# The pass for the maxima of the attention scores: 16 fills of two full matmuls, or 8 fills of four row tiles of 32 rows

## The chip, the cores and the metric

The kernel runs on one core of one Trainium2 chip. The metric is the device time of one execution in microseconds (us); three executions of the kernel before took 3145.16, 3150.84 and 3152.6 us, median 3150.84 us. The profile is of one execution more, whose own time is 3152.29 us and whose span, from the first to the last instruction, is 3150.6 us.

## The reference

A batch of 32 latent arrays of 64 x 256 (float32) passes through six residual layers; the context has 1601 keys of 256 values for each of the 32. The layers are a cross attention with one head, a causal self attention, a quantised feed-forward layer with a convolution, a cross attention with 16 heads, a causal self attention with 16 heads, and a mixture of 8 experts of which each token takes two. Only the fourth is touched here:

```python
def _L1_xattn_ref(x, mem, W_kv, W_q, W_proj, b_proj):
    kv = (mem @ W_kv).reshape(B, Nkv, 2, HEADS, HEAD_DIM)      # 16 heads of 16
    k = kv[:, :, 0].transpose(0, 2, 1, 3)
    v = kv[:, :, 1].transpose(0, 2, 1, 3)
    q = (x @ W_q).reshape(B, Nq, HEADS, HEAD_DIM).transpose(0, 2, 1, 3)
    attn = jnp.einsum('bhqd,bhkd->bhqk', q, k) * SCALE
    attn = jax.nn.softmax(attn, axis=-1)                       # over 1601 keys
    out = jnp.einsum('bhqk,bhkd->bhqd', attn, v)
    return out.transpose(0, 2, 1, 3).reshape(B, Nq, C) @ W_proj + b_proj
```

The softmax needs, for each of the 16 x 64 pairs of head and query of one batch element, a shift near the largest of 1601 scores. The kernel finds these maxima in a pass of its own (scores with one fp32r product, layout: queries on partitions), and then computes the scores again, accurately, with keys on partitions, for the exponentials.

## The kernel before

The 32 batch elements are worked on in 16 pairs; a pair is one trip (`pe_pair`) and each of its two elements is one call of `pe_batch(n, ...)`, n = 0 or 1. Trips 1 to 14 are one hardware loop (L1302); the first and the last stand outside it. The order of each engine's instructions is written out by hand, engine by engine, and semaphores tie them together.

One `pe_batch` on TensorE (L1237) is, in order:

1. waits for the split queries (`qbd_hi`, `qbd_lo`) and keys of this element and, where there is a next element, for its split context (`ctx_lo`);
2. the maxima stage, 16 units u. Unit u takes head pair u // 2 (2 heads x 64 queries = 128 output partitions) and one half of the keys: two matmuls (512 and about 290 columns) of 128 x 128 weights `qbd_hi`. These weights are block diagonal by head: in the 128 rows of a group of eight heads, head pair j has values only in rows 32 j to 32 j + 31, and zeros elsewhere. The output fills banks 0 and 1 or banks 2 and 3 in turn, so a unit waits for the reduction of the unit before the last (`mx_red >= u - 1`, L1137);
3. between the units stand the projections of the next element's keys and values (`project`, "pieces": 8 key pieces of 6 matmuls of 400 columns, then 7 value pieces, six of 12 and the last of 6 matmuls of 256 columns), twelve of the fifteen; the last tile of the weighted values of the element before (`weigh(1 - n, 12)`) after unit 0, and its denominators (`end_batch`, one matmul into bank 7) after unit 2;
4. a transposition of the maxima (`m8`, L1260 and L1261), the other three pieces, and then the wait for `shift` (L1267);
5. the scores stage: 13 tiles of keys (L1268), each with 2 + 12 matmuls in row tiles of 64 rows, the exponential on ScalarE, `weigh` (16 products in column tiles of 32 columns), and steps of the next layer (`finish`) and of the next pair (`prepare`).

`project` writes banks 6 and 5 in turn. ScalarE takes each piece out (`evac`, L749), and copies the sums of the weighted values (`copy_sums`) after the first piece.

VectorE in the maxima stage (`maxima`, L1619): for each unit it waits for `mx_ps`, reduces 802 or 799 columns of two banks to one column of `mpart` (L1626), and after unit 2 does `end_batch` (reciprocal L1614 and product L1616). Then it reduces `mpart` to `m8` (L1630), waits for its transposition, and builds `shift` (L1632 to L1642) for the scores.

Of the kernel before, what the change touches and what calls it, by code (L numbers as in the profile page):

```python
# [19 lines left out]
ALU = mybir.AluOpType  # L20
# [5 lines left out]
AX = mybir.AxisListType.X  # L26

P = 128
B, S, D = 32, 64, 256
NK = 1601  # L30
NKP = NK + 1
# [30 lines left out]

MAX_CHUNKS = [(0, 512), (512, HALF - 512), (HALF, 512), (HALF + 512, NKP - HALF - 512)]
PROJ_CHUNKS = [(0, HALF - 400), (HALF - 400, 400), (HALF, 400), (HALF + 400, NKP - HALF - 400)]
CTX_PARTS = 2
MAX_UNITS = 2 * PAIRS

K_PIECES = [("k", o, c) for o in range(KT) for c in range(len(PROJ_CHUNKS))]
V_PIECES = [("v", t, min(t + 2, KEY_TILES)) for t in range(0, KEY_TILES, 2)]
PIECES = K_PIECES + V_PIECES  # L70
PIECE_AFTER = (0, 2, 3, 4, 5, 7, 9, 10, 12, 13, 15)
CTX_STEPS = (1, 2, 6, 7)
# [43 lines left out]
def build(nc, io, out):  # L116
    ctx = ExitStack()
    with ctx:
# [91 lines left out]
        sideB = sb_b("sideB", [P, 3584])  # L210
        mpart = sb_b("mpart", [P, PAIRS, 2])
        sh8 = sb_b("sh8", [P, 2, P], BF16)
# [709 lines left out]
        def _(pe):  # L922
# [210 lines left out]
            def maxima(n, u):  # L1133

                pair, half = divmod(u, 2)
                if u >= 2:
                    pe.wait_ge(s.mx_red, T["mx"].now() + u - 1)  # L1137
                for c, width in MAX_CHUNKS[2 * half:2 * half + 2]:
                    at = 1024 * ((u + 1) % 2) + c - HALF * half
                    at = PS[:, at:at + width]  # L1140
                    mm = pe.matmul(at, qbd_hi[:, n, pair // 4, (pair % 4) * P:(pair % 4) * P + P], k_hi[:, n, pair // 4, c:c + width],  # L1141
                                   start=True, stop=True)
                mm.then_inc(s.mx_ps, 1)
# [15 lines left out]
            def end_batch(n, fin):  # L1159

                pe.wait_ge(s.sums_ready, T["sums"].up())
                if n == 0 and fin:
                    pe.wait_ge(s.p4T_ready, T["p4T"].now() + 1)
                pe.matmul(bank(7, D), spread[:, :, :].rearrange("p j d -> p (j d)"), sums_sb[:, :], start=True, stop=True).then_inc(s.den_ps, 1)
# [72 lines left out]
            def pe_batch(n, first, last):  # L1237
# [6 lines left out]
                if ahead:  # L1244
                    pe.wait_ge(s.ctx_lo_ready, T["ctxB"].up(KT * CTX_PARTS))
                for u in range(MAX_UNITS):
                    maxima(n, u)
                    if not (first and n == 0):
                        if u == 0:
                            weigh(1 - n, KEY_TILES - 1)  # L1250
                        if u == 2:
                            end_batch(1 - n, not first)
                    if ahead and u in PIECE_AFTER:
                        project(pieces.pop(0), 1 - n)
                T["mx"].up(MAX_UNITS)
                if ahead:
                    project(pieces.pop(0), 1 - n)

# [131 lines left out]
        def _(v):  # L1390
# [228 lines left out]
            def maxima(b, first):  # L1619

                for u in range(MAX_UNITS):
                    pair, half = divmod(u, 2)
                    width = HALF if half == 0 else NK - HALF
                    at = 1024 * ((u + 1) % 2)
                    v.wait_ge(s.mx_ps, T["mx"].up())
                    v.tensor_reduce(mpart[:, pair, half:half + 1], PS[:, at:at + width], AX, ALU.max).then_inc(s.mx_red, 1)  # L1626
                    if u == 2 and not (first and b == 0):
                        end_batch(1 - b)
                v.wait_ge(s.mx_red, T["mx"].now())
                v.tensor_reduce(m8[:, :, 0:PAIRS], mpart[:, None, :, :].broadcast_to([P, 4, PAIRS, 2]), AX, ALU.max).then_inc(s.m8_ready, 1)  # L1630
                v.wait_ge(s.m8T_ps, T["m8T"].up())
# [317 lines left out]
```

## Time and profile before

| | |
|---|---|
| median of three executions | 3150.84 us (3145.16 to 3152.6) |
| profiled execution, its own time | 3152.29 us |
| its span | 3150.6 us |
| mean granted TensorE clock | 0.918 of full speed |
| TensorE busy | 2665.3 us, 85% |
| VectorE busy | 1537.9 us, 49% |
| ScalarE busy | 1409.4 us, 45% |
| GpSimd busy | 926.9 us, 29% |
| part with the cross attention of 16 heads (first to last matmul of the maxima) | 689.3 to 2546.1 us |

Times in the rows are microseconds from the start of the span. "busy" of a matmul runs to its modelled end, which overlaps the next one's start; the step from one start to the next is the rate. PE is TensorE, PEld its weight loads, DVE VectorE, ACT ScalarE, POOL GpSimd. PEclk is the granted TensorE clock, 1.00 for 2.4 GHz and 0.50 for 1.2 GHz.

### The profile page before, as it was taken

What the parts mean: (1) busy time and instruction counts of PE and PEld (TensorE: products, weight loads), DVE (VectorE), ACT (ScalarE), POOL (GpSimd) and SP (SyncE); (2) the same over time, 40 slices, a digit from 0 to 9 for tenths busy, and PEclk for the clock granted to TensorE, in tenths of its full rate; (3) what the DMA queues carried; (4) which work ended last, traced back from release to release, by engine and by line L of the source; (5) the groups of instructions that cost most, each with busy time, mean ns of one, the idle gap of its engine ahead of it and who ended that gap; (6) DMA issues with size and microseconds to landing.
All of it is one profiled execution on the core that took longest, in us unless ns stands there. A gap on an engine that the chain in (4) does not pass through costs nothing.

```text
span 3150.6 us, 76656 instructions
## 1 busy us (share of the span) xinstructions
PE 2665.3 (85%) x31988; PEld 2234.6 (71%) x31988; DVE 1537.9 (49%) x2629; ACT 1409.4 (45%) x2563; POOL 926.9 (29%) x867
## 2 busy tenths in 40 slices
PE   6999722359999999999999999999999975499997
PEld 3555411158888888788788788788788854499997
DVE  3444477723543543444454344345345334377775
ACT  1222211136546546546545545545555521356554
POOL 1000043353333333333343342432433301312111
PEclk9999855679999999999999999999999975799999
DMA  8888400031001001001101100100110001466665
GB/s 340 314 322 320 162 0 0 7 120 44 23 23 44 22 23 37 29 23 33 34 23 33 34 23 22 44 23 22 34 33 22 13 2 55 160 210 201 204 206 151
DMA packets 48609, 270.65 MB, mean 86 GB/s; under 512 B 4896, under 2 KB 23584, under 8 KB 33696
## 3 DMA queue, kind: packets, MB, share of 16 engines
q1 hardware_dynamic: 40160, 255.82, 22.4%
q0 software_dynamic: 8160, 10.29, 2.1%
q8 instruction: 265, 4.34, 0.6%
q14 instruction: 24, 0.20, 0.0%
HBM read 247.58 MB, written 20.61 MB: 85 GB/s over the span
## 4 chain that ended last, share of the span: by engine, by line
issue 41%; PE 24%; POOL 21%; DVE 6%; DMA 5%; ACT 2%; POOLq 1%; SPq 0%; DVEq 0%; ACTq 0%
POOL k_lo L530 7%; POOL ctx_lo L538 6%; PE PS L1025 3%; PE PS L1005 3%; POOL sideB L558 2%; DMA sum_d<-scaled,xg 2%; DMA unit_raw<-in_experts 2%; POOL qbd_lo L543 2%; PE PS L1357 2%; PE PS L1358 1%; PE PS L1359 1%; PE PS L1277 1%; PE PS L1153 1%; POOL slots_d L633 1%; DVE small L1508 1%
## 5 line engine op out<-in xcount | busy, mean ns | idle before, releaser
L1626 DVE TENSOR_REDUCE mpart<-PS 128x1 f32<-128x802 f32 (+1 forms) x512 | 486.7, 987 | 549.4 <-PE PS L1141 549.4
L825 ACT ACTIVATE probs<-PS 128x1024 f32<-128x1024 f32 (+1 forms) x416 | 425.4, 1023 | 252.5 <-PE PS L1277 246.8
L530 POOL TENSOR_TENSOR k_lo<-sideB,k_hi 128x400 fp32r<-128x400 f32 (+1 forms) x256 | 252.2, 985 | 469.8 <-ACT k_hi L761 469.7
L538 POOL TENSOR_TENSOR ctx_lo<-ctx_raw,ctx_hi 128x801 fp32r<-128x801 f32 x128 | 224.4, 1763 | 459.1 <-ACT ctx_hi L773 459.0
L1141 PE MATMUL PS<-k_hi,qbd_hi 128*128 128x512 f32 (+2 forms) x1024 | 274.3, 371 | 85.6 <-issue 48.2
L1277 PE MATMUL PS<-qbd_hi,k_hi 64*128 64x256 f32 (+1 forms) x1664 | 312.9, 373 | 0.0
L760 ACT COPY sideB<-PS 128x400 f32<-128x400 f32 (+1 forms) x256 | 126.4, 494 | 364.5 <-PE PS L1121 355.0
L1153 PE MATMUL PS<-probs,vals 128*32 128x64 f32 x13312 | 277.9, 225 | 1.7 <-ACT probs L825 1.7
L1141 PEld LDWEIGHTS PS<-k_hi,qbd_hi 128*128 128x128 f32 x1024 | 184.6, 200 | 114.0 <-issue 77.7
L1153 PEld LDWEIGHTS PS<-probs,vals 128*32 128x32 f32 x13312 | 209.8, 112 | 67.0 <-issue 16.2
L1128 PE MATMUL PS<-wkv_hi,ctx_hi 128*128 128x256 f32 (+1 forms) x832 | 236.8, 285 | 0.0
L1277 PE MATMUL PS<-qbd_hi,k_lo 64*128 64x256 f32 (+1 forms) x1664 | 235.4, 279 | 0.0
L1277 PE MATMUL PS<-qbd_lo,k_hi 64*128 64x256 f32 (+1 forms) x1664 | 235.0, 279 | 0.1
L1130 PE MATMUL PS<-wkv_hi,ctx_lo 128*128 128x256 f32 (+1 forms) x832 | 234.7, 282 | 0.0
L1129 PE MATMUL PS<-wkv_lo,ctx_hi 128*128 128x256 f32 (+1 forms) x832 | 233.6, 281 | 0.0
L1357 PE MATMUL PS<-xT_hi,unit_hi 128*128 128x256 f32 x736 | 209.2, 284 | 3.3 <-DVE xT_lo L1832 3.0
L1119 PE MATMUL PS<-ctx_hi,wkv_hi 128*128 128x400 f32 (+1 forms) x512 | 194.1, 379 | 18.9 <-POOL ctx_lo L538 18.9
L1358 PE MATMUL PS<-xT_lo,unit_hi 128*128 128x256 f32 x736 | 209.2, 284 | 0.0
L763 ACT COPY vals<-PS 128x512 f32<-128x512 f32 x192 | 112.8, 588 | 214.4 <-PE PS L1130 214.4
L1359 PE MATMUL PS<-xT_hi,unit_lo 128*128 128x256 f32 x736 | 208.5, 283 | 0.0
L1120 PE MATMUL PS<-ctx_lo,wkv_hi 128*128 128x400 f32 (+1 forms) x512 | 183.5, 358 | 0.0
L1121 PE MATMUL PS<-ctx_hi,wkv_lo 128*128 128x400 f32 (+1 forms) x512 | 183.3, 358 | 0.0
(319 smaller groups left out, 6151.6 us busy)
## 6 DMA issues: line engine op xcount, KB each, us to landing
unit_raw<-in_experts SPq DMA_DIRECT2D x46, 1536.0 KB, 7.1
ctxN<-in_ctxN SPq DMA_DIRECT2D x16, 3328.0 KB, 10.9
ctxT<-in_ctxT SPq DMA_DIRECT2D x16, 3204.0 KB, 10.4
ctx_raw<-in_ctxT SPq DMA_DIRECT2D x64, 801.0 KB, 4.4
slots_d<-pad_rows SPq DMA_DIRECT2D x2, 2990.0 KB, 18.6
xg<-slots_d SPq DMA_DIRECT2D x23, 260.0 KB, 2.8
x<-in_x SPq DMA_DIRECT2D x1, 2048.0 KB, 10.3
sum_d<-x SPq DMA_DIRECT2D x1, 2048.0 KB, 6.3
```

Source lines behind the costliest of these rows:

```text
L530: g.tensor_tensor(k_lo[:, n, a, c:c + width], k_raw[p % 2][:, 0:width], k_hi[:, n, a, c:c + width].bitcast(F32), ALU.subtract).then_inc(s. ...
L538: g.tensor_tensor(ctx_lo[:, a, cols], ctx_raw[:, cols], ctx_hi[:, a, cols].bitcast(F32), ALU.subtract).then_inc(s.ctx_lo_ready, 1)
L825: act.activation(probs[rows, t % PROBS, :], PS[rows, 1024 * (t % 2):1024 * (t % 2) + 1024], ACT.Exp).then_inc(s.pr_ready, 1)
L1128: pe.matmul(to, ctx_hi[:, k, keys], wkv_hi[:, k, D:2 * D], start=k == 0, stop=False)
L1130: mm = pe.matmul(to, ctx_lo[:, k, keys], wkv_hi[:, k, D:2 * D], start=False, stop=k == KT - 1)
L1141: mm = pe.matmul(at, qbd_hi[:, n, pair // 4, (pair % 4) * P:(pair % 4) * P + P], k_hi[:, n, pair // 4, c:c + width], start=True, stop=True)
L1153: mm = pe.matmul(bank(4, S, slice(32 * j, 32 * j + 32), g * S), vals[rows, n, mine:mine + 32], probs[rows, t % PROBS, at_head(h):at_head(h ...
L1277: mm = pe.matmul(bank(2 * (t % 2) + r, 256, rows, a * 256), keys_part[part, n, a, keys], queries[part, n, a, r * 256:r * 256 + 256], start ...
L1357: pe.matmul(to, hi[:, k, cols], tokens_hi[:, k, :], start=k == 0, stop=False)
L1358: pe.matmul(to, hi[:, k, cols], tokens_lo[:, k, :], start=False, stop=False)
L1359: mm = pe.matmul(to, lo[:, k, cols], tokens_hi[:, k, :], start=False, stop=k == KT - 1)
L1626: v.tensor_reduce(mpart[:, pair, half:half + 1], PS[:, at:at + width], AX, ALU.max).then_inc(s.mx_red, 1)
```

## The change

The maxima stage has 8 units instead of 16. Unit u takes a group a = u // 4 of eight heads and a quarter part = u % 4 of the keys (`PROJ_CHUNKS`: 402, 400, 400, 400 columns). Its four matmuls have 32 rows of weights each, rows 32 j to 32 j + 31 for head pair j, the only rows where that pair's weights are not zero, and write banks 0 to 3. One VectorE instruction then reduces all four banks to four columns of `mpart`. Every unit uses all four banks, so unit u waits for the reduction of unit u - 1.

The first piece and the last `weigh` of the element before now stand ahead of unit 0 and two waits are added ahead of them (`x_done`, `cat_ready`, since the piece writes bank 6); `end_batch` stands after unit 1; ten pieces stand after the units (1, 1, 1, 2, 1, 2, 1, 1), and the four that are left stand after the transposition of the maxima.

```diff
-MAX_CHUNKS = [(0, 512), (512, HALF - 512), (HALF, 512), (HALF + 512, NKP - HALF - 512)]
 PROJ_CHUNKS = [(0, HALF - 400), (HALF - 400, 400), (HALF, 400), (HALF + 400, NKP - HALF - 400)]
-MAX_UNITS = 2 * PAIRS
+MAX_UNITS = 8
-PIECE_AFTER = (0, 2, 3, 4, 5, 7, 9, 10, 12, 13, 15)
+PIECES_AFTER = (1, 1, 1, 2, 1, 2, 1, 1)
-        mpart = sb_b("mpart", [P, PAIRS, 2])
+        mpart = sb_b("mpart", [P, PAIRS, 4])
             def maxima(n, u):
-                pair, half = divmod(u, 2)
-                if u >= 2:
-                    pe.wait_ge(s.mx_red, T["mx"].now() + u - 1)
-                for c, width in MAX_CHUNKS[2 * half:2 * half + 2]:
-                    at = 1024 * ((u + 1) % 2) + c - HALF * half
-                    at = PS[:, at:at + width]
-                    mm = pe.matmul(at, qbd_hi[:, n, pair // 4, (pair % 4) * P:(pair % 4) * P + P], k_hi[:, n, pair // 4, c:c + width],
-                                   start=True, stop=True)
+                a, part = divmod(u, 4)
+                if u:
+                    pe.wait_ge(s.mx_red, T["mx"].now() + u)
+                c, width = PROJ_CHUNKS[part]
+                for j in range(4):
+                    rows = slice(32 * j, 32 * j + 32)
+                    mm = pe.matmul(bank(j, width), qbd_hi[rows, n, a, j * P:j * P + P], k_hi[rows, n, a, c:c + width], start=True, stop=True)
                 mm.then_inc(s.mx_ps, 1)
@@ pe_batch
+                if n == 0 and not first:
+                    pe.wait_ge(s.x_done, T["x_done"].now())
+                if n == 1 and not first:
+                    pe.wait_ge(s.cat_ready, T["cat"].now() + 1)
+                if ahead:
+                    project(pieces.pop(0), 1 - n)
+                if not (first and n == 0):
+                    weigh(1 - n, KEY_TILES - 1)
                 for u in range(MAX_UNITS):
                     maxima(n, u)
-                    if not (first and n == 0):
-                        if u == 0:
-                            weigh(1 - n, KEY_TILES - 1)
-                        if u == 2:
-                            end_batch(1 - n, not first)
-                    if ahead and u in PIECE_AFTER:
-                        project(pieces.pop(0), 1 - n)
+                    if u == 1 and not (first and n == 0):
+                        end_batch(1 - n, not first)
+                    if ahead:
+                        for _ in range(PIECES_AFTER[u]):
+                            project(pieces.pop(0), 1 - n)
                 T["mx"].up(MAX_UNITS)
-                if ahead:
-                    project(pieces.pop(0), 1 - n)
@@ maxima on VectorE
-                    pair, half = divmod(u, 2)
-                    width = HALF if half == 0 else NK - HALF
-                    at = 1024 * ((u + 1) % 2)
+                    a, part = divmod(u, 4)
+                    width = min(PROJ_CHUNKS[part][1], NK - PROJ_CHUNKS[part][0])
                     v.wait_ge(s.mx_ps, T["mx"].up())
-                    v.tensor_reduce(mpart[:, pair, half:half + 1], PS[:, at:at + width], AX, ALU.max).then_inc(s.mx_red, 1)
-                    if u == 2 and not (first and b == 0):
+                    v.tensor_reduce(mpart[:, 4 * a:4 * a + 4, part], PS[:, 0:2048].rearrange("p (j x) -> p j x", j=4)[:, :, 0:width],
+                                    AX, ALU.max).then_inc(s.mx_red, 1)
+                    if u == 1 and not (first and b == 0):
                         end_batch(1 - b)
                 v.wait_ge(s.mx_red, T["mx"].now())
-                v.tensor_reduce(m8[:, :, 0:PAIRS], mpart[:, None, :, :].broadcast_to([P, 4, PAIRS, 2]), AX, ALU.max).then_inc(s.m8_ready, 1)
+                v.tensor_reduce(m8[:, :, 0:PAIRS], mpart[:, None, :, :].broadcast_to([P, 4, PAIRS, 4]), AX, ALU.max).then_inc(s.m8_ready, 1)
```

## Rows read from the trace of the kernel before

**Rows 1.** Page, groups of instructions: count, busy, mean ns, idle before and its releaser.
```profile
L1626 DVE TENSOR_REDUCE mpart<-PS 128x1 f32<-128x802 f32 (+1 forms) x512 | 486.7, 987 | 549.4 <-PE PS L1141 549.4
```

**Rows 2.** Instructions in time, PE, one n = 1 element: start, duration, what, idle before.
```profile
1571.98 0.62 PE L1141 MATMUL PS<-k_hi,qbd_hi 128*128 128x512 f32 x2
1572.53 0.65 PE L1153 MATMUL PS<-probs,vals 65*32 65x64 f32 x32
1573.12 0.46 PE L1119 MATMUL PS<-ctx_hi,wkv_hi 128*128 128x402 f32 x1
...
1574.32 0.89 PE L1141 MATMUL PS<-k_hi,qbd_hi 128*128 128x512 f32 x4
...
1578.83 0.53 PE L1141 MATMUL PS<-k_hi,qbd_hi 128*128 128x512 f32 x2
1579.19 0.35 PE L1119 MATMUL PS<-ctx_hi,wkv_hi 128*128 128x400 f32 x1
...
1580.30 0.52 PE L1141 MATMUL PS<-k_hi,qbd_hi 128*128 128x512 f32 x2
...
1588.03 0.28 PE L1128 MATMUL PS<-wkv_hi,ctx_hi 128*128 128x256 f32 x1
...
1589.46 0.53 PE L1141 MATMUL PS<-k_hi,qbd_hi 128*128 128x512 f32 x2
```

**Rows 3.** Instructions in time, DVE, the same element.
```profile
1572.64 0.99 DVE L1626 TENSOR_REDUCE mpart<-PS 128x1 f32<-128x802 f32 x1 [2.29 <-PE PS L1141]
...
1576.69 1.75 DVE L1614 RECIPROCAL inv<-PS 128x256 f32<-128x256 f32 x1
...
1578.81 1.88 DVE L1626 TENSOR_REDUCE mpart<-PS 128x1 f32<-128x799 f32 x2
...
1591.82 1.89 DVE L1626 TENSOR_REDUCE mpart<-PS 128x1 f32<-128x802 f32 x2 [0.80 <-PE PS L1141]
1593.74 0.22 DVE L1630 TENSOR_REDUCE m<-mpart 128x32 f32<-128x64 f32 x1
1595.32 0.29 DVE L1632 TENSOR_SCALAR sh<-PS 128x128 bf16<-128x128 f32 x1 [1.35 <-PE PS L1261]
```

**Rows 4.** Instructions in time, PE, the end of the same stage.
```profile
1594.83 0.28 PE L1260 MATMUL PS<-ones 128*128 128x1 f32 x2
...
1599.13 0.39 PE L1273 MATMUL PS<-shift,onesb 64*128 64x512 bf16 x2 [0.31 <-DVE shift L1642]
```

**Rows 5.** Instructions in time, PE and DVE, the n = 0 element that follows.
```profile
1629.20 1.03 PE L1141 MATMUL PS<-k_hi,qbd_hi 128*128 128x512 f32 x2 [4.83 <-issue]
...
1631.18 0.70 PE L1119 MATMUL PS<-ctx_hi,wkv_hi 128*128 128x402 f32 x1
...
1633.35 1.54 PE L1141 MATMUL PS<-k_hi,qbd_hi 128*128 128x512 f32 x4
...
1658.79 0.39 PE L1273 MATMUL PS<-shift,onesb 64*128 64x512 bf16 x2 [0.31 <-DVE shift L1642]
...
1630.27 0.99 DVE L1626 TENSOR_REDUCE mpart<-PS 128x1 f32<-128x802 f32 x1 [20.57 <-PE PS L1141]
```

**Rows 6.** Instructions in time, PE, scores stage: pairs of row tiles of 64 rows.
```profile
1601.50 0.28 PE L1277 MATMUL PS<-qbd_lo,k_hi 64*128 64x256 f32 x2
1601.62 0.28 PE L1277 MATMUL PS<-qbd_hi,k_lo 64*128 64x256 f32 x2
```

**Rows 7.** Instructions in time, DVE: a reduction to four columns.
```profile
1567.81 0.69 DVE L1667 TENSOR_REDUCE small<-sideB 128x4 f32<-128x512 f32 x1
```

**Rows 8.** Windows: us, busy (instructions) of PE, PEld, DVE, ACT, POOL; PEclk; DMA share, GB/s.
```profile
1572.00:1595.00 23.00, 22.33 (x168) 20.65 (x166) 17.47 (x19) 9.85 (x22) 7.99 (x8) 1.00 0.01 1
1629.00:1636.00 7.00, 6.79 (x47) 5.42 (x48) 2.73 (x3) 1.17 (x3) 1.03 (x1) 0.51 0.01 2
2538.00:2540.00 2.00, 1.82 (x5) 0.98 (x4) 1.85 (x2) 0.00 (x0) 0.00 (x0) 0.50 0.00 0
```

**Rows 9.** Instructions in time, PE, the last element, which has no pieces.
```profile
2535.28 0.63 PE L1141 MATMUL PS<-k_hi,qbd_hi 128*128 128x512 f32 x2 [2.39 <-DVE mpart L1626]
```

## The prediction, made before the changed kernel ran

> **What bounds the kernel now.** I read the page's groups first. The reductions of the maxima on VectorE are its costliest group, 512 instructions, and VectorE idles 549.4 us in front of them, waiting for TensorE's fills [rows 1]; this says that TensorE leads in the stage, and no more, for most of that idle time is the scores stage ahead of each first fill. So I read the instructions in time through one maxima stage. In an n = 1 element the stage runs from 1571.98 (first fill) to 1599.13 (first matmul of the scores) [rows 2, 4], 27.15 us. TensorE is dense there: 22.33 us busy of 23.00, at the full clock [rows 8]. VectorE is busy 17.47 of those 23 us, so it is the second limit and not far behind: its last reduction ends at 1593.71, the maxima are ready at 1593.96 [rows 3], and TensorE gets to their transposition only at 1594.83 [rows 4], because pieces stand ahead of it. After the transposition the order turns round: TensorE waits 0.31 us for VectorE's `shift` [rows 4]. In an n = 0 element the stage starts after 4.83 us without a matmul and runs at half clock at first (0.51 over 7 us [rows 8]); it takes 1658.79 - 1629.20 = 29.59 us [rows 5].
>
> **The change, part by part.** Price list at full clock. A unit's fill of two matmuls takes TensorE 1579.19 - 1578.83 = 0.36 us; a key piece 1580.30 - 1579.19 = 1.11 us; a value piece 1589.46 - 1588.03 = 1.43 us, 0.119 for each of its 12 matmuls; the first piece after `weigh` 1574.32 - 1573.12 = 1.20; `weigh` 1573.12 - 1572.53 = 0.59 [rows 2]. From the start of a lone fill to the start of its reduction: 1572.64 - 1571.98 = 0.66 [rows 2, 3]. A reduction of 802 elements takes 0.99 alone and 0.92 back to back (0.99 + 0.92 give the 1.89 of two) [rows 3].
>
> *TensorE's work.* Removed: 16 fills, 5.8 us. Added: 8 fills of four matmuls. The trace has no row tile of 32 rows. It has pairs of row tiles of 64 rows: two matmuls of 256 columns start every 0.12 us [rows 6], where one after the other at the piece's rate (0.119 for 256 columns) would need 0.24. So row tiles run side by side and their weight loads keep up. One fill then lies between 0.18 us (all four side by side, 1.11 / 6 for 400 columns) and 0.74 (none); by the pairs' row I take 0.25. Eight make 2.0 us. Each fill also switches the array from 128 rows to row tiles and back. What a switch costs I read from the piece behind `weigh`: 1.20 against 1.11, about 0.1 us; the bound from below is nothing. 16 switches make 1.6 us. TensorE's work falls by 5.8 - 2.0 - 1.6 = 2.2 us for each element.
>
> *VectorE's work.* 802 elements take 0.99 [rows 3] and 512 elements in four groups 0.69 [rows 7], so 1.03 ns for each element more and nothing visible for groups. 1600 elements: 0.99 + 0.8 x 1.03 = 1.82 us; the bounds are 1.70 and 1.84, the latter twice the back-to-back 0.92. Eight make 14.6 us against 16 x 0.92 = 14.7. VectorE gains nothing.
>
> *The buffers.* This is the part that decides. Before, two halves of the four banks alternate and a fill lies beside a reduction. After, every fill uses all four banks: fill, reduction and fill stand in series. One round is a hop to TensorE (0.05), fill to reduction start, and 1.82. For the middle term: 0.66 is with two matmuls in series, 0.48 with one (less 0.18), and three more row tiles add 0 to 0.17 (three more weight loads at half of the 0.12 of a pair); with no overlap it is 0.48 + 3 x 0.18 = 1.03. I take 0.57. A round is 2.44 us, in which TensorE has 0.25 + 0.1 + 1.11 + 0.1 = 1.56 us to do where one piece stands behind the fill. So VectorE with its fills becomes the limit, and TensorE waits about 0.9 us in a round.
>
> *The sum for n = 1,* from the start of the stage. First piece and `weigh`, now ahead of unit 0: 1.20 + 0.59 = 1.79; VectorE has nothing to do in them, where before its first reduction started at 0.66. Eight rounds without the first hop: 8 x 2.39 + 7 x 0.05 = 19.47. `end_batch` after unit 1: from its reciprocal to the next reduction 1578.81 - 1576.69 = 2.12 [rows 3], which takes the place of one gap of 0.62: 1.50. Two pieces stand behind units 3 and 5: 0.25 + 0.1 + 2.22 + 0.1 = 2.67 and, with one value piece, 2.99, over a round of 2.44: 0.2 + 0.5 = 0.7. The last reduction ends at 1.79 + 19.47 + 1.50 + 0.70 = 23.5 (before: 21.7). `m8` has twice the input, 0.22 + 0.07 [rows 3]; at 23.8 TensorE starts the transposition, which it now waits for (before: 22.85). Then four pieces instead of three, 42 matmuls x 0.119 = 5.0, and 0.2 for the transposition and 0.1 for a switch: scores at 29.1. VectorE's chain to `shift`, 1599.13 - 1594.83 = 4.3 [rows 4], ends earlier, at 28.1, so here the fourth piece is late instead. The change costs 29.1 - 27.15 = 2.0 us.
>
> *n = 0.* The first piece and `weigh` now run at half clock: 1633.35 - 1631.18 = 2.17 [rows 5] and 1.0 (between 0.59 and twice that, since the small products of `weigh` do not all follow the clock). Fill to reduction start at half clock is 1630.27 - 1629.20 = 1.07 less one matmul of 0.33 = 0.74 [rows 5]. The first reduction starts at 3.2 + 0.74 = 3.9 instead of 2.36, 1.6 later than in n = 1: scores at 29.1 + 1.6 = 30.7 against 29.59, 1.1 us more.
>
> *Ends.* The first element (no `weigh`, no `end_batch`) about 1.5. The last has no pieces; before, its 16 reductions stand almost back to back, and eight rounds at half clock (2.61) with their gaps cost about 3. Total 15 x 2.0 + 15 x 1.1 + 1.5 + 3 = 51 us. Added to the profiled execution's own 3152.3 this is 3203; that execution lies 1.5 us above the median of the three, which does not matter here.
>
> *What costs nothing.* The added waits: `cat_ready` asks for a product that VectorE did one or two key tiles earlier, `x_done` for one of ten tiles earlier; behind each stands the whole of TensorE's queue, so an error here would cost every element its length. The 0.53 us that TensorE waited for the copied sums goes, but off the limit. ScalarE (9.85 busy of 23) and GpSimd (7.99) [rows 8] follow the pieces at 1 us each.
>
> *A rule of the skill.* That TensorE's gain is lost in emptying the banks is what rows 3 give above. The Trainium skill, TensorEngine Tiling, "PSUM Bottleneck", says that tiling speeds up TensorE but not the emptying of PSUM, which may then be the limit; the row agrees, 0.99 us for 802 elements whatever filled them. The Trainium skill, TensorE: Matmul & The Clock Gate, "The mechanism", puts row tiles 4 ns apart; by it fill to reduction start would be 0.49, an estimate of 0.6 us less for each element and 3184 in all. No row here shows four tiles, so the sum stays at 0.57.
>
> **The rivals.**
>
> *A, faster: TensorE stays the limit.* If the rounds were short enough to fit TensorE's work, its 2.2 us saved would count and the 0.5 of the wait for the sums: 31 x 2.5 = 78, 3075 us. The place is the gap between two reductions; it decides when a round is below about 2.1 us. For it: TensorE is the dense engine now. Against it: a reduction alone is 1.82 by two rows, and a matmul's pipeline from start to release is 0.48 before anything is added.
>
> *B, the clock.* After unit 2's fill and piece TensorE has nothing until the reduction behind `end_batch`: about 2.4 us idle. In the last element before there is such a hole, 2.39 us [rows 9], and the granted clock is 0.50 in the stretch behind it [rows 8], the lower level, 1.2 GHz, and stays there with fills alone. With pieces around it TensorE is busier than there, which speaks against. If it falls, two key pieces behind unit 3 take 4.3 instead of 2.2, a delay of about 2 us for each element: 3203 + 31 x 2 = 3265.
>
> *C, four tiles do not run side by side.* Then fill to reduction start is 1.03: 8 x 0.46 x 32 = 118 more, 3321. Rows 6 show it for two tiles only.
>
> *D, the last part of the stage is mis-sized* (reduction of 1.70, tiles at 0.48, switches at nothing): 8 x (0.12 + 0.09) = 1.7 and 0.2 less for each element, 3203 - 60 = 3143, no change. It needs all bounds at one end.
>
> **How the numbers follow.** Forecast 0.55, A 0.12, B 0.17, C 0.06, D 0.10. The time is 3203. Its own range, with the fill at 0.48 to 0.65 and the reduction at 1.75 to 1.84, is 3203 - 37 to 3203 + 25. Towards B (holes that fall in some of the elements only) the range goes to 3270; downwards to 3155, which leaves out A, C and a part of D. A measurement can tell about 0.3% (9 us) from no change. Faster: A and a third of D, 0.15. Same: a third of D and an edge of the forecast, 0.06. Slower: 0.79.
>
> **What would show it.** In the changed profile: reductions of 1.82 us with 0.6 us gaps before them put down to the fills of the maxima; waits of about 0.9 us of TensorE for `mpart`; four row tiles starting within 0.25 us; fill 0 about 1.8 us (n = 1) and 3.2 us (n = 0) into the stage; the scores 29.1 and 30.7 us after its start; no wait for `shift`; granted clock 1.00 through the n = 1 stage. A shorter gap or reduction shows A or D, a clock of 0.5 behind `end_batch` shows B, starts 0.18 us apart show C.

## The result, and the profile after

The changed kernel takes 3245.9 us (median of four, 3242.7 to 3248.6) against 3151.2, a ratio of 1.030 (95% interval 1.029 to 1.032): 3% slower. The forecast was 3203 within 3155 to 3270, slower with a chance of 0.79. The direction came as forecast, and so did the main mechanism, fill and reduction in series; the size was 95 us against 51, and most of the difference comes from the clock.

The page of the changed kernel, groups of instructions (columns as in [rows 1], which the first of these answers to):

```profile
L1627 DVE TENSOR_REDUCE mpart<-PS 128x4 f32<-128x1600 f32 (+2 forms) x256 | 467.4, 1826 | 656.4 <-PE PS L1140 656.4
...
L1140 PE MATMUL PS<-k_hi,qbd_hi 32*128 32x400 f32 (+1 forms) x1024 | 128.6, 491 | 119.5 <-DVE mpart L1627 119.4
```

VectorE does half the instructions at twice the length: 467 us busy against 487. The new row is the second. TensorE idles 119.4 us in front of the fills, and what releases it is the reduction. Before, its idle time there was a turn of the loop and 8 us of reductions.

Instructions in time, VectorE, in an n = 1 element of the changed kernel (answers to [rows 3]); its stage starts at 1617.30:

```profile
1619.65 1.83 DVE L1627 TENSOR_REDUCE mpart<-PS 128x4 f32<-128x1608 f32 x1 [3.99 <-PE PS L1140]
1622.05 1.83 DVE L1627 TENSOR_REDUCE mpart<-PS 128x4 f32<-128x1600 f32 x1 [0.56 <-PE PS L1140]
1623.79 1.75 DVE L1616 RECIPROCAL inv<-PS 128x256 f32<-128x256 f32 x1
...
1625.91 1.82 DVE L1627 TENSOR_REDUCE mpart<-PS 128x4 f32<-128x1600 f32 x1
1628.29 1.82 DVE L1627 TENSOR_REDUCE mpart<-PS 128x4 f32<-128x1596 f32 x1 [0.56 <-PE PS L1140]
...
1638.95 1.82 DVE L1627 TENSOR_REDUCE mpart<-PS 128x4 f32<-128x1596 f32 x1 [0.56 <-PE PS L1140]
1640.80 0.28 DVE L1632 TENSOR_REDUCE m<-mpart 128x32 f32<-128x128 f32 x1
```

Every reduction but the one behind `end_batch` (1625.91) has at least 0.56 us in front of it in which VectorE waits for a fill that could not start before the last reduction had ended; behind a double piece it is 0.97 and 1.26. A round is 1628.29 - 1625.91 = 2.38 us.

The same element on TensorE, fills alone:

```profile
1621.54 0.46 PE L1140 MATMUL PS<-k_hi,qbd_hi 32*128 32x400 f32 x4 [0.66 <-DVE mpart L1627]
1621.92 0.70 PE L1162 MATMUL PS<-sums,spread 128*128 128x256 f32 x2
...
1623.93 0.46 PE L1140 MATMUL PS<-k_hi,qbd_hi 32*128 32x400 f32 x4 [0.21 <-DVE mpart L1627]
...
1627.79 0.46 PE L1140 MATMUL PS<-k_hi,qbd_hi 32*128 32x400 f32 x4 [2.09 <-DVE mpart L1627]
```

Four matmuls of 400 columns fit in 0.38 us from their start to the next instruction (1621.54 to 1621.92), where two plain ones of together about 800 columns need 0.36 [rows 2]: the four row tiles do run side by side. The last row is the wait behind `end_batch`, which matters below.

The end of the stage in an n = 0 element (answers to [rows 4]):

```profile
1578.03 0.38 PE L1262 MATMUL PS<-ones 128*128 128x1 f32 x2 [0.62 <-DVE m L1632]
...
1583.48 0.39 PE L1275 MATMUL PS<-shift,onesb 64*128 64x512 bf16 x2
```

TensorE now waits for the maxima (0.62 us) and no longer for `shift`; between the two rows lie 5.45 us, 4.30 before.

Windows over whole stages, from the first piece to the first matmul of the scores. First the kernel before, n = 1 and n = 0:

```profile
1571.98:1599.13 27.15, 26.17 (x199) 24.24 (x198) 21.09 (x30) 11.91 (x26) 7.99 (x8) 1.00 0.00 1
1629.20:1658.79 29.59, 29.12 (x197) 26.61 (x198) 21.07 (x29) 11.20 (x24) 7.77 (x8) 0.89 0.01 1
```

and the changed kernel, two n = 1 and two n = 0 elements:

```profile
1617.30:1646.59 29.29, 24.73 (x199) 20.46 (x199) 20.66 (x22) 11.64 (x25) 7.77 (x8) 1.00 0.01 1
2249.58:2280.39 30.81, 26.23 (x200) 21.75 (x199) 20.67 (x22) 11.64 (x25) 7.78 (x8) 0.94 0.00 1
1676.51:1709.76 33.25, 29.47 (x195) 24.10 (x197) 20.88 (x21) 11.01 (x23) 7.76 (x8) 0.83 0.00 1
2310.45:2342.01 31.56, 28.45 (x195) 23.34 (x196) 20.49 (x21) 11.02 (x23) 7.97 (x8) 0.86 0.00 1
```

The same stage comes in several lengths, and the clock (the column after the five engines) goes with them. Added over all 32 elements, the stages are 896.1 us before and 992.4 after. The 992.4 count the last element, which has no pieces, from its first fill; with the `weigh` ahead of it, which before lay inside the stage, they are 993.0, 96.9 more. The spans differ by 96.3, so next to nothing moved outside the stages. Of the 96.9, n = 1 has 45.6 and n = 0 51.3. Of the n = 1 elements without the last, 15 in all, 8 are 29.3 us at clock 1.00 and 7 are 30.4 to 30.9 us at 0.94.

Windows of 2 us in the n = 0 element that starts at 1550.21, and the fill and the piece there:

```profile
1554.00:1556.00 2.00, 2.00 (x10) 1.83 (x6) 1.72 (x1) 0.03 (x1) 0.63 (x1) 0.50 0.00 0
...
1558.00:1560.00 2.00, 2.00 (x13) 1.49 (x13) 2.00 (x2) 0.58 (x2) 0.43 (x1) 1.00 0.00 0
1560.00:1562.00 2.00, 1.01 (x6) 0.68 (x4) 1.97 (x3) 1.19 (x3) 0.89 (x1) 1.00 0.00 0
1562.00:1564.00 2.00, 0.66 (x5) 0.46 (x6) 1.44 (x2) 0.01 (x1) 0.90 (x1) 1.00 0.00 0
1564.00:1566.00 2.00, 2.00 (x9) 1.99 (x9) 1.68 (x1) 0.63 (x2) 0.00 (x0) 0.70 0.00 0
1566.00:1568.00 2.00, 2.00 (x9) 1.19 (x9) 0.05 (x1) 0.89 (x3) 0.90 (x1) 0.50 0.00 0
```

```profile
1563.34 0.46 PE L1140 MATMUL PS<-k_hi,qbd_hi 32*128 32x400 f32 x4 [2.33 <-DVE mpart L1627]
...
1564.57 0.35 PE L1119 MATMUL PS<-ctx_lo,wkv_hi 128*128 128x402 f32 x1
...
1565.38 0.54 PE L1119 MATMUL PS<-ctx_lo,wkv_hi 128*128 128x400 f32 x1
```

TensorE had been idle 2.33 us; 1.5 us after it is back at work the clock falls from 2.4 to 1.2 GHz (0.54 for the matmul that took 0.35), and the two key pieces behind unit 3 run at half rate. The clock is low twice in this element: at its start, after the turn of the loop, and here. Over all elements with `end_batch` the second low stretch is seen in 7 of 15 n = 1 elements and in 11 of 15 n = 0 elements; "hit" below means such a stretch. Where it begins differs, from the last part of the wait itself to 1.7 us behind it.

### The profile page after: what moved, and what is told of

The parts are those of the page before. It is cut to its first block, busy times and chain, and to the rows that moved or that the text cites. A ratio compares the mean times of both kernels' runs of the same rounds, so it can differ in the third digit from the quotient of the medians.

```text
span 3246.9 us, 75907 instructions
## 1 busy us (share of the span) xinstructions
PE 2653.3 (82%) x31984; PEld 2143.6 (66%) x31988; DVE 1518.9 (47%) x2373; ACT 1411.3 (43%) x2563; POOL 924.6 (28%) x867
## 4 chain that ended last, share of the span: by engine, by line
issue 42%; PE 26%; POOL 20%; DVE 7%; DMA 3%; ACT 2%; POOLq 1%; SPq 0%; DVEq 0%; ACTq 0%
POOL k_lo L529 6%; POOL ctx_lo L537 6%; PE PS L1024 3%; PE PS L1004 3%; PE PS L1359 2%; PE PS L1360 2%; PE PS L1361 2%; POOL sideB L557 2%; DVE mpart L1627 2%; POOL qbd_lo L542 2%; DMA unit_raw<-in_experts 1%; PE PS L1279 1%; PE PS L1376 1%; PE PS L1378 1%; PE PS L1377 1%
## 5 line engine op out<-in xcount | busy, mean ns | idle before, releaser
L1627 DVE TENSOR_REDUCE mpart<-PS 128x4 f32<-128x1600 f32 (+2 forms) x256 | 467.4, 1826 | 656.4 <-PE PS L1140 656.4
L1118 PE MATMUL PS<-ctx_hi,wkv_hi 128*128 128x400 f32 (+1 forms) x512 | 228.4, 446 | 94.9 <-issue 53.2
L1140 PE MATMUL PS<-k_hi,qbd_hi 32*128 32x400 f32 (+1 forms) x1024 | 128.6, 491 | 119.5 <-DVE mpart L1627 119.4
L1118 PEld LDWEIGHTS PS<-ctx_hi,wkv_hi 128*128 128x128 f32 x512 | 111.8, 218 | 134.8 <-issue 128.0
L1119 PE MATMUL PS<-ctx_lo,wkv_hi 128*128 128x400 f32 (+1 forms) x512 | 198.4, 388 | 0.0
L1120 PE MATMUL PS<-ctx_hi,wkv_lo 128*128 128x400 f32 (+1 forms) x512 | 198.2, 387 | 0.0
```

Source lines behind the costliest of these rows:

```text
L1118: pe.matmul(bank(at, width), wkv_hi[:, k, cols], ctx_hi[:, k, c:c + width], start=k == 0, stop=False)
L1627: v.tensor_reduce(mpart[:, 4 * a:4 * a + 4, part], PS[:, 0:2048].rearrange("p (j x) -> p j x", j=4)[:, :, 0:width], AX, ALU.max).then_inc( ...
```

## The experiments

"Stages" are the sums over the 32 elements, read from instructions in time; the changed kernel has 992.4, the kernel before 896.1 (in the changed kernel and those made from it the last element is counted from its first fill). The medians are of 4 to 11 runs, beside the kernel before on the same chip (medians 3148.0 to 3150.0 us).

**Pieces into the wait behind `end_batch` (e1_hole).**

```diff
-PIECES_AFTER = (1, 1, 1, 2, 1, 2, 1, 1)
+PIECES_AFTER = (1, 1, 2, 1, 1, 2, 1, 1)
```

> Change: the pieces behind the eight units are (1,1,2,1,1,2,1,1) instead of (1,1,1,2,1,2,1,1), so two key pieces, 2.2 us, stand in front of the wait for the reduction that VectorE does only after end_batch; that wait was 2.33 us. Theory (the clock falls because of this hole, and costs about 1.6 us in some 20 of the 32 elements): the granted clock stays at 1.00 in the n = 1 stages and after the start of the n = 0 stages, and unit 3 no longer overruns its round by 0.4 us: 3246 - 20 x 1.6 - 30 x 0.4 = about 3202 us. Rival (the clock falls because the whole stage is less dense, or because of the row tiles, wherever the pieces stand): only the 0.4 us go, about 3234 us, and low clock is still seen in the stage.

Measured 3220.7 us (expected 3202, by the rival 3234), stages 963.3. The stage without a fall of the clock is 28.9 instead of 29.3, as expected. Three of 15 n = 1 elements (7 in the changed kernel) are still hit, at 29.6 to 31.2 us, and 12 of the 13 n = 0 elements behind a full turn of the loop are 31.1 to 31.9. So it lies between the two theories: the wait, 1.0 us instead of 2.1, still does harm at times, and the n = 0 elements did not lose what was expected.

**Matmuls that nobody reads, in that wait (e4_dummy).**

```diff
+                        if u == 2:
+                            pe.wait_ge(s.k_hi_ready, T["k_sb"].now() + 3)
+                            for _ in range(12):
+                                pe.matmul(bank(6, 256), wkv_hi[:, 0, 0:P], wkv_hi[:, 0, 0:256], start=True, stop=True)
```

> Change: in the changed kernel, twelve matmuls whose result nobody reads (256 columns, into the free bank 6, about 1.4 us at full clock) are added after the piece behind unit 2, in the wait for the reduction after end_batch. Nothing else moves. Theory (the hole makes the clock fall): although work is added, the low clock in the stages goes and the time falls by 20 x 1.6 us, to about 3213 us; unit 3 keeps its overrun of 0.4 us. Rival (the clock does not depend on this hole): 3246 us or a little more.

Measured 3205.2 us: 41 us less, with 372 matmuls added. In time on TensorE, and a whole n = 1 stage as a window:

```profile
1607.57 1.58 PE L1262 MATMUL PS<-wkv_hi 128*128 128x256 f32 x12
1609.81 0.46 PE L1140 MATMUL PS<-k_hi,qbd_hi 32*128 32x400 f32 x4 [0.67 <-DVE mpart L1631]
```

```profile
1599.33:1628.63 29.30, 26.18 (x210) 22.02 (x208) 20.67 (x22) 11.64 (x25) 7.77 (x8) 1.00 0.00 1
```

All 15 n = 1 elements are 29.3 us at clock 1.00, no one is hit. Nor is an n = 0 element hit behind the wait. The stages are 966.3, 26 less. Another 13 us lie outside the stages: the 14 stretches from an n = 1 element's scores to the next stage, 13 of them with a full turn of the loop, took 402.7 us in all against 415.4. The control shows what those are.

**The same matmuls elsewhere (e9_ctl).** Six behind unit 4 and six behind unit 6:

```diff
+                        if u in (4, 6):
...
+                            for _ in range(6):
+                                pe.matmul(bank(5 if u == 4 else 6, 256), wkv_hi[:, 0, 0:P], wkv_hi[:, 0, 0:256], start=True, stop=True)
```

> Control for e4_dummy: the same twelve matmuls that nobody reads for each element, so the same count of instructions, but six behind the piece of unit 4 and six behind that of unit 6, where TensorE waits only 0.5 to 0.8 us; the wait of 2.3 us behind end_batch stays open. Theory (e4_dummy was faster because its matmuls stood in the long wait): part of the n = 1 elements still show a stretch at half clock in the stage, as in the changed kernel, and the stages are not shorter than the changed kernel's 992 us in all; the time is 3246 us, less up to 14 us if the loop's turn, 30.0 us from scores to the next stage in the changed kernel and 29.0 in e4_dummy, goes with the count of instructions. Rival (any added matmuls keep the clock up, wherever they stand): stages of about 966 us in all and about 3205 us.

Measured 3242.6 us, stages 1003.5; the same 14 stretches took 402.8, as in e4_dummy. One n = 1 element, TensorE and the window:

```profile
1751.39 0.46 PE L1140 MATMUL PS<-k_hi,qbd_hi 32*128 32x400 f32 x4 [2.11 <-DVE mpart L1634]
1755.58 0.55 PE L1140 MATMUL PS<-k_hi,qbd_hi 32*128 32x402 f32 x4
```

```profile
1740.90:1772.05 31.15, 27.54 (x211) 23.30 (x210) 20.68 (x22) 11.64 (x25) 7.80 (x8) 0.95 0.01 1
```

13 of 15 n = 1 elements are hit (31.1 us at 0.95 against 29.7 at 1.00). So 13 us of e4_dummy's gain come with the added matmuls wherever they stand, and their place is worth 1003.5 - 966.3 = 37 us of stages. About 10 of these are rounds that the added matmuls make late here (29.7 against 29.3 at clock 1.00, 30 elements); the other 27 are what the open wait behind `end_batch` costs, 19 of them in the 13 n = 1 elements.

The 13 us are the idle time of TensorE at the turn. The first matmul of an n = 0 stage behind it, in the changed kernel and in e4_dummy:

```profile
1676.51 0.70 PE L1118 MATMUL PS<-ctx_hi,wkv_hi 128*128 128x402 f32 x1 [4.68 <-issue]
```

```profile
1657.85 0.70 PE L1118 MATMUL PS<-ctx_hi,wkv_hi 128*128 128x402 f32 x1 [3.97 <-POOL qbd_lo L542]
```

Over 13 turns the idle time is 4.77 us on average in the changed kernel and 3.80 and 3.81 in the two with added matmuls; all the rest of the stretch takes 25.24 us in each of the three. In the changed kernel TensorE mostly starts over a microsecond after its last input, `qbd_lo`, is there, and the profile puts the wait down to nothing but its own issue (11 of 13); with the added matmuls it starts 0.0 to 0.5 us after `qbd_lo`, which now ends the wait.

**A longer wait (e10_big), and the changed kernel again (a2_same).**

```diff
-PIECES_AFTER = (1, 1, 1, 2, 1, 2, 1, 1)
+PIECES_AFTER = (1, 2, 0, 2, 1, 2, 1, 1)
```

> Change against the changed kernel: the piece behind unit 2 stands behind unit 1 instead (pieces 1,2,0,2,1,2,1,1), where VectorE is busy with end_batch anyway; TensorE's amount of work and VectorE's row are the same, but TensorE's wait behind end_batch is one stretch of about 2.7 to 3.3 us instead of 2.3. Theory (a long enough wait makes the clock fall): more elements are hit, all n = 1 stages are 30.8 us or more instead of 6 or 7 of 15, about 3246 + 9 x 1.6 = 3260 us. Rival (the clock looks at the amount of work in the stage, not at one wait): the same as the changed kernel, 3246 us.

> The changed kernel once more, for a second trace: how many of its n = 1 elements are 29.3 us and how many 30.4 to 30.9. Theory (the fall of the clock hangs on how the wait behind end_batch lies against something that the kernel does not set): another number of elements is hit than the 6 of 15 in the first trace, and each hit costs 1.1 to 1.7 us. Rival (it hangs on the data or on the place in the program): the same elements are hit again.

e10_big measured 3251.1 us, stages 1002.1, with waits of 2.56 us; 11 of 15 n = 1 elements are hit, not all, so the expectation failed in its strong form. a2_same measured 3245.8 us and has 10 of 15 hit; the first n = 1 element is hit in the first trace and not in the second, the third the other way round. So the same program at the same place is hit or not: the place in the program alone does not decide a single case. A wait of 2.6 us cannot be told from one of 2.1 by these counts.

**All 128 rows (e2_full).**

```diff
-                    rows = slice(32 * j, 32 * j + 32)
-                    mm = pe.matmul(bank(j, width), qbd_hi[rows, n, a, j * P:j * P + P], k_hi[rows, n, a, c:c + width], start=True, stop=True)
+                    mm = pe.matmul(bank(j, width), qbd_hi[:, n, a, j * P:j * P + P], k_hi[:, n, a, c:c + width], start=True, stop=True)
```

> Change: same eight units, banks and reductions, but each of the four matmuls of a unit has all 128 rows of weights (96 of them zeros) instead of 32, so the four run one after the other. Theory (four row tiles run side by side and shorten the gap between two reductions): fill to reduction start rises from 0.51 to about 1.06 us, 8 x 0.55 = 4.4 us for each element, 3246 + 32 x 4.4 = about 3386 us, less up to 33 us if the denser stage keeps the clock up. Rival (the row tiles bring nothing, the changed kernel's 0.51 us is latency): within 10 us of 3246.

Measured 3335.2 us. VectorE in time:

```profile
1669.27 1.82 DVE L1626 TENSOR_REDUCE mpart<-PS 128x4 f32<-128x1596 f32 x1 [1.09 <-PE PS L1139]
```

The gap is 1.09 instead of 0.56, so the four tiles take 0.53 us out of a round. n = 1 stages are 32.3 at clock 1.00 against 29.3, 3.0 more and not 4.4: `end_batch` covers one gap of eight, and the two behind double pieces were late anyway (1.11 and 1.46 us against 0.97 and 1.26). These 1.4 us in 30 elements are the larger part of what the time is under the expected 3386.

This kernel turned out to bear on two other steps. Its wait behind `end_batch` is 1.8 us, and 6 of its 15 n = 1 elements are hit, such as this one, 33.8 us against 32.3:

```profile
1787.18:1820.98 33.80, 28.65 (x198) 26.30 (x197) 20.68 (x22) 11.63 (x25) 7.77 (x8) 0.95 0.00 1
```

So the fall behind the wait does not need row tiles. The slow start does differ: over the first 12 us of the 13 n = 0 stages that follow a full turn of the loop, its TensorE spends 5.7 us at half clock on average; the changed kernel, with the same order of work, 8.0.

**Three pieces behind the transposition (e3_tail).**

```diff
-PIECES_AFTER = (1, 1, 1, 2, 1, 2, 1, 1)
+PIECES_AFTER = (1, 1, 1, 2, 1, 2, 1, 2)
```

> Change: two pieces instead of one behind unit 7, so three pieces instead of four stand behind the transposition of the maxima. Theory (the last part of the stage is set by TensorE's four pieces, 5.4 us, where VectorE's chain to the shift needs 4.3): the transposition is 0.65 us later, the rest 1.15 shorter, 31 x 0.5 = 15 us less, about 3231 us, and TensorE again waits for the shift. Rival (the transposition's place is what counts, VectorE's chain hangs on it): 0.65 later and nothing back, about 3266 us.

Measured 3233.2 us (expected 3231). An n = 1 stage at clock 1.00 is 28.8 instead of 29.3, the 0.5 that was expected. 11 of 15 n = 1 elements are hit here, at 29.9 to 31.3 us, with the same wait of 2.1 us, so the total came close to the forecast with more falls in n = 1 than in the changed kernel and, as the stages of n = 0 show (499 us against 516), with less lost there.

**Nothing ahead of unit 0 but `weigh` (e5_first), and both together (e7_combo).**

```diff
-PIECES_AFTER = (1, 1, 1, 2, 1, 2, 1, 1)
+PIECES_AFTER = (1, 1, 3, 1, 1, 2, 1, 1)     # e7_combo: (1, 1, 3, 1, 1, 2, 1, 2)
-                if ahead:
-                    project(pieces.pop(0), 1 - n)
                 if not (first and n == 0):
                     weigh(1 - n, KEY_TILES - 1)
```

> Change against the kernel e1_hole: the first piece no longer stands ahead of unit 0 but behind unit 2, in what is left of the hole (pieces 1,1,3,1,1,2,1,1 behind the units and none ahead; weigh stays ahead). Theory (VectorE's row of fills and reductions is the limit, so what stands ahead of unit 0 counts in full, and what stands in the hole counts nothing): n = 1 stages 28.9 - 1.15 = 27.75 us, n = 0 stages 31.2 - 2.0 = 29.2, in all 3221 - 15 x 1.15 - 15 x 2.0 = about 3174 us. Rival (TensorE's amount of work sets the stage, wherever it stands): no change against e1_hole, 3221 us.

> Change against e5_first: a second piece behind unit 7, so three instead of four pieces stand behind the transposition. Theory: as in e3_tail, 0.45 us less for each element, e5_first less 14 us, about 3160 us, which is still not faster than the kernel before (3148). Rival: the denser order makes TensorE the limit and nothing more comes, within 5 us of e5_first.

Measured 3194.4 and 3179.8 us. Windows from the first fill, so without `weigh` (0.6 us, 1.1 at half clock), e5_first n = 0 and n = 1, then e7_combo n = 1:

```profile
1649.48:1679.92 30.44, 27.59 (x168) 22.46 (x165) 20.68 (x21) 10.91 (x23) 7.75 (x8) 0.86 0.00 1
1714.52:1741.82 27.30, 24.25 (x170) 19.99 (x165) 20.77 (x22) 11.01 (x24) 7.73 (x8) 1.00 0.00 1
```

```profile
1711.13:1737.89 26.76, 24.03 (x170) 19.91 (x165) 20.62 (x22) 11.29 (x25) 7.73 (x8) 1.00 0.01 1
```

n = 1 with `weigh` is 27.9 (28.9 in e1_hole, expected 27.75) and 27.4 in e7_combo: nearly the 27.15 of before. No n = 1 element is hit in either. n = 0 gained 0.9 us, not 2.0 (with `weigh` the sum of its stages is 484.2, against 497.6), 0.7 behind a full turn of the loop, where the clock stays low at the start. The rival, no change, is out; the step for n = 0 was wrong. Of the 14.6 us between e5_first and e7_combo only 5 lie in the stages (929.9 and 924.7, with `weigh`): n = 1 gives 8 back and n = 0 takes 3, with 9.9 us at half clock in its first 12 against 8.1. So e7_combo's 14 us came at the expected size only with differences outside the stages, which the change does not touch.

**Row tiles alone, on two pairs of banks in turn (e6_two).** In the kernel before, with its order and its 16 units:

```diff
-                for c, width in MAX_CHUNKS[2 * half:2 * half + 2]:
...
+                a, part = divmod(u // 2, 4)
+                c, width = PROJ_CHUNKS[part]
+                for i in range(2):
+                    j = 2 * (u % 2) + i
+                    rows = slice(32 * j, 32 * j + 32)
+                    mm = pe.matmul(bank(2 * ((u + 1) % 2) + i, width), qbd_hi[rows, n, a, j * P:j * P + P], k_hi[rows, n, a, c:c + width],
```

> Change against the kernel before: only row tiles, with its 16 units, two pairs of banks in turn, its order of pieces and its reductions of about 800 elements; a unit is now two row tiles of 32 rows (two head pairs, 400 columns each) into the two banks, instead of one head pair by two chunks. Theory (what costs in the changed kernel is that fill and reduction stand in series over one set of four banks; a fill of row tiles costs TensorE about 0.45 to 0.5 us with both switches, against 0.36): VectorE has no gap of 0.56 us put down to a fill that had to wait for it, TensorE is dense in the stage, and the stage is longer than before by 16 x 0.1 to 0.14 = 1.4 to 2.3 us: 3148 + 31 x 1.4 to 2.3 = 3190 to 3220 us. Rival (the switches cost nothing where the array is dense, and two tiles side by side save 0.15 us a unit): 27.15 - 2.2 is below VectorE's row, so stages of about 25.5 to 26.5 and 3100 to 3130 us.

Measured 3182.4 us, stages 928.4. Fills on TensorE in an n = 1 element, one key piece between each two, and the window of another:

```profile
1596.71 0.45 PE L1142 MATMUL PS<-k_hi,qbd_hi 32*128 32x400 f32 x2
1598.38 0.45 PE L1142 MATMUL PS<-k_hi,qbd_hi 32*128 32x400 f32 x2
1600.06 0.45 PE L1142 MATMUL PS<-k_hi,qbd_hi 32*128 32x400 f32 x2
```

```profile
1714.40:1742.13 27.73, 26.24 (x197) 20.98 (x197) 21.13 (x30) 11.78 (x25) 8.01 (x8) 1.00 0.00 1
```

A round of fill and piece is 1.67 us; before it is 1580.30 - 1578.83 = 1.47 [rows 2]. So two row tiles of 32 rows cost TensorE 0.56 us with both switches, where two plain matmuls of 128 rows cost 0.36. Two fills in a row, four tiles, cost the same 0.56, where four plain matmuls cost 0.72, so only a lone fill loses; the expectation charged all sixteen, and 3190 was too high. Alternation brings n = 1 from 29.3 to 27.7, and TensorE waits for a reduction once in the stage, 0.31 us. That the 0.6 us left over 27.15 are the price of the switches fits these numbers but was not tested by itself. n = 0 stays at 31.2 (29.5 before) at clock 0.85. The last element, without pieces and so without switches between its fills, is 22.3 us against 24.15: there the tiles do gain. In the first 12 us of an n = 0 stage TensorE is at half clock for 9.5 us on average, against 5.4 in the kernel before.

**`end_batch` one unit later in the kernel before (e8_late).**

```diff
-                        if u == 2:
+                        if u == 3:
                             end_batch(1 - n, not first)
```

and the same on VectorE.

> Change against the kernel before: end_batch stands after unit 3 instead of unit 2 on TensorE and VectorE, nothing else. TensorE waits 0.53 us there for the copied sums. Theory (in the kernel before TensorE's dense row sets the maxima stage): the wait goes and the stage is 0.5 us shorter, 31 x 0.5 = 15 us, about 3133 us. Rival (VectorE's row is already as long, and the part behind the transposition takes the gain): within 6 us of 3148.

Measured 3142.4 us, ratio to the kernel before 0.998 (0.997 to 0.999): 6 us faster, the only version here that beats both kernels. n = 1 is 27.0 instead of 27.15; n = 0 behind a full turn, though, is 28.8 on average instead of 29.5. The 0.5 us expected in n = 1 did not come: TensorE now waits twice for a reduction, 0.53 us together, so VectorE's row was as long, as the rival said.

```profile
1576.95 0.63 PE L1141 MATMUL PS<-k_hi,qbd_hi 128*128 128x512 f32 x2 [0.26 <-DVE mpart L1626]
1577.85 0.63 PE L1141 MATMUL PS<-k_hi,qbd_hi 128*128 128x512 f32 x2 [0.27 <-DVE mpart L1626]
```

What came, came with the clock (4.0 us at half clock in the first 12 of an n = 0 stage, 5.4 before).

## Why the prediction was right, and where not

- *The rounds.* Forecast: 0.57 from fill to reduction start, 1.82 for the reduction, round 2.44. Measured 0.51, 1.83 and 2.38. TensorE's saving had nowhere to go because fill and reduction stand in series. e2_full shows that the gap is a term of the sum, e6_two that alternation takes TensorE's wait for the reductions away but for 0.31 us.
- *TensorE's work.* 5.8 less 2.0 less 1.6 was 2.2 us saved. A fill with both switches costs 0.56 us for two tiles; for four, 0.38 to the next instruction, 0.1 more until that one's second matmul and 0.1 ahead of the fill, about 0.58. Eight cost 4.6, so the saving was 1.2, about half of it. It hardly counts, since TensorE waits in the changed kernel, 0.65 us in a round with one piece where 0.9 were forecast.
- *n = 1.* Last reduction ends at 23.5 (forecast 23.5), scores at 29.3 (29.1): 2.15 us more (2.0) where the clock holds. The fourth piece behind the transposition was late, as forecast, and e3_tail gave the 0.5 us back. The granted clock of 1.00 through the stage, which the prediction named as a sign, was seen in 8 of 15.
- *The step that failed: the clock.* The sum had no term for a fall behind `end_batch`, and it let the slow start of n = 0 last as long as before. The 97 us of stages are 46 more than the 51 forecast. By the lengths with and without a low stretch, about 29 of the 46 are falls behind `end_batch`: 10 in the 7 n = 1 elements and 19 in n = 0, where a stage is 33.3 us with a second fall and 31.6 without. About 13 are the slow start: in the 13 elements behind a full turn the stage is 2.1 us longer than before even without a second fall (31.6 against 29.5 on average), where 1.1 were forecast. These splits are estimates from the rows; e4_dummy against e9_ctl gives 27 us for the falls by another way.
- *Rival B* (0.17) was named with its place and its price, the wait behind `end_batch` and 2 us, and that is what these falls are. The prediction widened its range for holes that fall in some of the elements, and the measured time is in the stated range by that alone: it lies outside the forecast's own 3166 to 3228 (whose lower end should be 3162, since 8 x 0.16 x 32 is 41 and not 37). What was missing is B as a term of the sum with a share of the cases. It cost 1.1 to 1.6 us in 7 of 15 n = 1 elements and 1.3 to 2.4 in 11 of 15 in n = 0. e4_dummy against e9_ctl settles it: twelve matmuls without use in that wait are 37 us faster than in other places, 27 of them by the clock. By the Trainium skill, TensorE: Matmul & The Clock Gate, "HAM oscillation — how this bites in real kernels", idle stretches between bursts of matmuls put the clock back to half rate; these rows agree, and add that one wait of 2.1 us in an otherwise busy stage does it in 7 to 13 of 15 cases.
- *The slow start of n = 0.* How long the clock stays low after the loop's turn is not given from outside but depends on what TensorE does. From the windows, 2 x (1 - PEclk) x 12 us, averaged over 13 stages: 5.4 us before, 5.7 in e2_full and 4.0 in e8_late, which have no row tiles in the maxima; 8.0 in the changed kernel (7.5 in its second trace), 9.5 in e6_two, and 7.8 to 9.9 in the seven other kernels, which have. The first 12 us of such a stage as windows, one kernel after the other: before, e6_two, e2_full and the changed kernel:

```profile
1870.07:1882.07 12.00, 11.53 (x76) 9.93 (x77) 7.94 (x8) 3.84 (x9) 3.43 (x4) 0.80 0.01 1
```

```profile
1894.92:1906.92 12.00, 11.38 (x68) 8.37 (x68) 7.00 (x7) 2.94 (x7) 2.32 (x3) 0.61 0.01 1
```

```profile
1981.65:1993.65 12.00, 11.08 (x70) 9.37 (x70) 5.82 (x5) 3.04 (x7) 2.83 (x3) 0.76 0.01 1
```

```profile
1171.04:1183.04 12.00, 10.91 (x70) 8.12 (x70) 6.79 (x5) 3.93 (x9) 2.83 (x4) 0.66 0.00 1
```

Two pairs have the same order of work and differ in the fills (before and e6_two; e2_full and the changed kernel), and both say the same: fills in row tiles of 32 rows keep the clock low for 2.3 to 4.1 us more of these 12 (1.7 with the second trace). Counted whole, with the part that lies ahead of the stage, the low stretch is 6.3 us on average before and in e2_full, 10.0 in the changed kernel (9.4 in its second trace) and 10.2 in e6_two. That is shown; why is not. It does not follow TensorE's busy time alone: in the 12 us e1_hole is busy 12.0 us on average and at half clock for 8.9, e2_full 11.1 and 5.7. The tiles also change the weight loads and how many rows of the array work at a time, and no run separates these.
- *Rivals A, C and D* are out: the round is 2.38, over the 2.1 from which A decides; e2_full shows what C would have been (measured 3335, forecast for C 3321); and D needed a reduction of 1.70 and switches at nothing, where 1.83 and about 0.1 us each were measured.
- *The ends.* The last element was forecast at 3 us and cost 3.3 with its `weigh`, the first at 1.5 and cost 1.3.

## What to carry to other kernels

Before widening an operation over all the buffers it has, count the buffers that are left: here half the instructions bought a fill and a reduction in series, and the engine that was relieved was not the one that then mattered. Write the new wait beside TensorE's order and see how long the longest idle stretch becomes; moving real work into it can be worth more than the time it takes up, because behind an open wait the clock may run at half rate. And treat such a clock effect as a term with a share of the cases, and the length of a slow start as something the change can lengthen, not as given.

## What the runs showed of the hardware that was not expected

- Row tiles of 32 rows run fully side by side: two or four of them take the same 0.38 us to the next instruction. But a fill of them between dense matmuls of 128 rows costs 0.2 us more than these 0.38 (1.67 us for fill and piece, against 1.47 with two plain matmuls), so at 400 columns two tiles lose against two plain matmuls, and four win against four (0.56 against 0.72 us).
- Adding twelve matmuls for each element to the loop's program made TensorE's idle time at each of 13 turns of the loop 1.0 us shorter (3.8 against 4.8 us), in both places tried. The two programs share the added matmuls and a wait or two beside them; why this shortens the turn was not tested.
- Row tiles of 32 rows in the slow start delay the return of the full clock: 7.5 to 9.9 us at half clock in the first 12 in ten traces with them, against 4.0 to 5.7 in three without. The two pairs that differ in the fills (e2_full and the changed kernel, before and e6_two) are among them.
- The fall of the clock behind the longest wait of the stage, counted in the 15 n = 1 elements: 7, 10, 11 and 13 of 15 where it is 2.1 us (changed kernel twice, e3_tail, e9_ctl), 11 at 2.6 (e10_big), 6 at 1.8 (e2_full), 3 at 1.0 (e1_hole) and none where no wait is over 0.9 (e4_dummy, e5_first, e7_combo, e6_two).
